# Graph kernel on one core: the first layer's segment sums with 64-column one-hot weights in two column tiles, edge values streamed, sums transposed back, and both one-hots from one operation

## What is computed

```python
z2 = jnp.concatenate([node_feat[src], node_feat[dst], edge_feat], axis=-1)
e = jax.nn.relu(z2 @ W_pre + b_pre)                 # 128 values an edge
deg = jax.ops.segment_sum(jnp.ones((e.shape[0],), e.dtype), dst, num_segments=N)
s = jax.ops.segment_sum(e, dst, num_segments=N)
mean_sq = jax.ops.segment_sum(e * e, dst, num_segments=N) / safe_deg
mx = jax.ops.segment_max(e, dst, num_segments=N)
mn = jax.ops.segment_min(e, dst, num_segments=N)
```

## Time and profile before

| | |
|---|---|
| median of 3 runs | 7895.94 us (7865.68 to 7899.78) |
| the profiled execution's own time | 7904.27 us, its span 7902.4 us |
| TensorE matmul busy | 5956.0 us (75%) |
| TensorE weight load busy | 5083.7 us (64%) |
| VectorE busy | 4835.5 us (61%) |
| ScalarE busy | 2658.9 us (34%) |
| GpSimd busy | 3831.2 us (48%) |
| mean granted TensorE clock | 0.79 |
| DMA | 541.35 MB |

### The profile page before, as it was taken

How to read it: one execution, slowest core, us unless ns; L and a number is a source line. 1 busy time by engine, 2 the same in 40 slices (tenths; PEclk the granted TensorE clock), 3 DMA queues, 4 the chain that set the end, 5 groups by cost and what they waited for, 6 DMA issues and landing times. The chain is left out here.

```text
span 7902.4 us, 163825 instructions
## 1 busy us (share of the span) xinstructions
PE 5956.0 (75%) x38014; PEld 5083.7 (64%) x38014; DVE 4835.5 (61%) x13892; ACT 2658.9 (34%) x5907; POOL 3831.2 (48%) x3975
## 2 busy tenths in 40 slices
PE   4888888888888888856767665667777676766674
PEld 4888888888888888435655553555555555555554
DVE  4666666666666666655555454556655565555557
ACT  1333333333333333212222233333333333333335
POOL 3455555545554544035555524555555555555552
PEclk7999999999999999968888776665666666666666
DMA  5444444444444444311111111111111111111111
GB/s 130 110 111 110 109 109 110 111 109 109 110 111 109 109 110 107 94 44 39 40 39 38 37 30 37 36 39 37 38 37 39 37 38 37 38 37 37 37 39 42
DMA packets 608470, 541.35 MB, mean 69 GB/s; under 512 B 307553, under 2 KB 485930, under 8 KB 608081
## 3 DMA queue, kind: packets, MB, share of 16 engines
q0 software_dynamic: 126192, 261.30, 13.9%
q1 hardware_dynamic: 356874, 163.66, 9.0%
q10 hardware_dynamic: 125272, 115.10, 5.5%
HBM read 517.22 MB, written 22.31 MB: 68 GB/s over the span
## 5 line engine op out<-in xcount | busy, mean ns | idle before, releaser
L1674 POOL DMA_INDIRECT Gt<-TAB,metat x1632 | 1586.4, 972 | 1522.5 <-DMA ad<-ADT 751.7
L520 POOL DMA_INDIRECT G<-Atab,meta x1616 | 1529.3, 946 | 1534.8 <-DVE EE L555 831.2
L659 PE MATMUL S<-oh,EE 128*128 128x64 f32 x6464 | 824.7, 280 | 218.7 <-DVE acc L586 110.8
L659 PEld LDWEIGHTS S<-oh,EE 128*128 128x128 f32 x6464 | 779.4, 196 | 283.1 <-DVE acc L586 155.6
L1166 POOL DMA_INDIRECT Gc<-XS,metac x672 | 650.0, 967 | 576.9 <-PE Sc L1336 294.5
L624 ACT COPY BS<-BK 128x512 f32<-128x512 f32 x404 | 237.0, 587 | 1861.5 <-PE BK L669 1630.5
L680 PE MATMUL S<-ohl,BS 128*128 128x64 f32 x6464 | 783.6, 274 | 6.2 <-issue 4.0
L680 PEld LDWEIGHTS S<-ohl,BS 128*128 128x128 f32 x6464 | 775.4, 195 | 13.6 <-issue 12.2
L555 DVE TENSOR_TENSOR EE<-Z,G 128x512 f32<-128x512 f32 x404 | 279.4, 692 | 783.6 <-remote 747.5
L1869 PE MATMUL SR<-P,Gt 128*128 128x128 f32 x3264 | 746.5, 400 | 0.0
L1869 PEld LDWEIGHTS SR<-P,Gt 128*128 128x128 f32 x3264 | 636.9, 291 | 114.7 <-issue 114.7
(11 more groups left out here) (269 smaller groups left out, 11712.6 us busy)
## 6 DMA issues: line engine op xcount, KB each, us to landing
mm<-MM ACTq DMA_DIRECT2D x404, 256.0 KB
ZR<-in_eft SPq DMA_DIRECT2D x404, 128.0 KB
dstb<-in_lin SPq DMA_DIRECT2D x404, 128.0 KB
Gt<-TAB,metat POOLq DMA_INDIRECT x1632
G<-Atab,meta POOLq DMA_INDIRECT x1616
ad<-ADT SPq DMA_DIRECT2D x816, 0.2 KB
WB<-Btab SPq DMA_DIRECT2D x404, 32.0 KB
Gc<-XS,metac POOLq DMA_INDIRECT x672
```

The costliest lines, as they stand in the source:

```text
L520: e.indirect_dma_start(G[:, k, s, :], None, Atab, bass.IndirectOffsetOnAxis(ap=meta[:, k, s:s + 1], axis=0)).then_inc(l_g[k], 16)
L659: mm = e.matmul(S1[:, a * W:(a + 1) * W], lhs, rhs, start=(s == 0), stop=(s == 3))
L1674: e.indirect_dma_start(G[:, k, s, :], None, TAB, bass.IndirectOffsetOnAxis(ap=meta[:, k, s:s + 1], axis=0)).then_inc(l_g[k], 16)
```

## The change

The one-hot becomes the stationary operand (64 columns) and 128 edge values are streamed. The values' sums go to partitions 0 to 63 of PSUM and the squares' to 64 to 127, as do the maximum and minimum, so two column halves of the array are used in turn. The results then have nodes on the partitions; ScalarE copies them to `SN1`/`SN2` (`e1`, `e2`), TensorE transposes them back (`t1`, `t2`), and VectorE adds the transposed block to `acc` as before. The one-hot of last edges comes from a number that the setup writes to a new table `MD`: the destination, lowered by 65536 where the next edge has the same one. One operation (`hot`, 512 columns) then makes both one-hots. `meta` is loaded in two parts. The order of stages changes on VectorE, ScalarE and TensorE, and `p4` moves from lag 6 to lag 5.

```diff
@@ setup, ScalarE
                                 vo[0:n, :, :]).then_inc(p_vo, 16)
+                    e.dma_start(MD[g * 128:g * 128 + n, :, :], mc[0:n, g % 2, :, :]).then_inc(p_md, 16)
                     if g < 2:
+                        e.wait_ge(p_md, 16 * (g + 1))
                         chunks(g + 2)
@@ setup, VectorE, each of four groups
+                    eq = hl[0:n, 0, :].rearrange("c (p s) -> c p s", s=4)
+                    ch(e.tensor_tensor(eq, mc[0:n, q, :, 4:8], mc[0:n, q, :, 8:12], ALU.is_equal))
+                    ch.sync()
+                    ch(e.scalar_tensor_tensor(mc[0:n, q, :, 8:12], eq, -65536.0, mc[0:n, q, :, 4:8],
+                                              ALU.mult, ALU.add))
@@ loads, SyncE
                 if not j.first(4):
-                    wait_sync(e, l_g[k], before[0], s_sync)
-                    wait_sync(e, s_d1, before[1], s_sync)
-                e.dma_start(meta[:, k, :], src[0]).then_inc(l_mt[k], 16)
+                    wait_sync(e, l_g[k], gathered, s_sync)
+                e.dma_start(ms[:, k, :], src[0]).then_inc(l_ms[k], 16)
...
+                if not j.first(4):
+                    wait_sync(e, s_zr, done, s_sync)
+                e.dma_start(dstb[64:128, k, :], src[4]).then_inc(l_db[k], 16)
+                if not j.first(4):
+                    wait_sync(e, s_oh, done, s_sync)
+                e.dma_start(md[:, k, :], src[1]).then_inc(l_md[k], 16)
@@ VectorE
-            def last(j):
+            def hot(j):
                 k = j.slot(4)
+                wait(e, l_md[k], 16 * j.uses(4))
                 if not j.first(4):
                     wait(e, s_p4, j.at(-3))
-                wait(e, s_d1, j.at(1))
-                e.tensor_tensor(ohl[:, k, :, :], oh[:, k, :, :], neq[:, k, :].unsqueeze(2).to_broadcast([128, 4, W]),
-                                ALU.mult).then_inc(s_ohl, 1)
+                e.scalar_tensor_tensor(oh[:, k, :, :], iotaW[:, :].unsqueeze(1).to_broadcast([128, 8, W]),
+                                       baseF[:, ds(j.at(), 1)],
+                                       md[:, k, :].unsqueeze(2).to_broadcast([128, 8, W]),
+                                       ALU.add, ALU.is_equal).then_inc(s_oh, 1)
...
-            pipeline(e, T, U, D, [(7, d4b), (2, d2), (0, d1), (3, last), (4, d4a), (4, d3)])
+            pipeline(e, T, U, D, [(2, d2), (0, d1), (6, d4b), (4, d4a), (2, hot), (4, d3)])
@@ ScalarE: e1 and e2 are new, the cast of oh comes last in a1
+                e.copy(SN1[:, :], S1[:, 0:128]).then_inc(s_e1, 1)
...
+                e.copy(SN2[:, :], S2[:, 0:128]).then_inc(s_e2, 1)
-            pipeline(e, T, U, D, [(5, a2), (1, masks), (2, a1)])
+            pipeline(e, T, U, D, [(5, a2), (1, masks), (2, a1), (3, e1), (5, e2)])
@@ TensorE
-                for a in range(3):
-                    for s in range(4):
-                        lhs = EE[:, q, a, s * 128:(s + 1) * 128] if a < 2 else onesb[:, :]
-                        rhs = oh[:, k, s, :] if a < 2 else ohb[:, q, s, :]
-                        mm = e.matmul(S1[:, a * W:(a + 1) * W], lhs, rhs, start=(s == 0), stop=(s == 3))
+                for s in range(4):
+                    e.matmul(S1[:, 256:256 + W], onesb[:, :], ohb[:, q, s, :], start=(s == 0), stop=(s == 3))
+                for s in range(4):
+                    for a in range(2):
+                        mm = e.matmul(S1[a * 64:(a + 1) * 64, 0:128], oh[:, k, s, :], EE[:, q, a, s * 128:(s + 1) * 128],
+                                      start=(s == 0), stop=(s == 3))
...
+            def t1(j):
+                wait(e, s_e1, j.at(1))
+                e.transpose(S1[:, 128:256], SN1[:, :], ident[:, :]).then_inc(s_t1, 1)
...
-            pipeline(e, T, U, D, [(5, p3), (1, p1), (6, p4), (3, p2)])
+            pipeline(e, T, U, D, [(5, p3), (6, t2), (4, t1), (1, p1), (3, p2), (5, p4)])
```

More of the change, by code:

```diff
@@ L440, in phase_l0 @@
         EE = sbt(ph, "EE", [128, 2, 2, CH])
-        oh = sbt(ph, "oh", [128, 4, 4, W])
+        oh = sbt(ph, "oh", [128, 4, 8, W])
         ohb = sbt(ph, "ohb", [128, 2, 4, W], BF16)
-        ohl = sbt(ph, "ohl", [128, 4, 4, W])
-        neq = sbt(ph, "neq", [128, 4, 4])
-        iob = sbt(ph, "iob", [128, 2, W])
         ST = sbt(ph, "ST", [128, 2, 2, CH])
         BS = sbt(ph, "BS", [128, 2, 2, CH])
+        SN1 = sbt(ph, "SN1", [128, 128])
+        SN2 = sbt(ph, "SN2", [128, 128])
         Z = [pst(ph, f"Z{k}", [128, CH]) for k in range(2)]
@@ L452, in phase_l0 @@
         BK = [pst(ph, f"BK{k}", [128, CH]) for k in range(2)]
-        S1v = S1[:, 0:3 * W].rearrange("p (a n) -> p a n", a=3)
-        S2v = S2[:, 0:2 * W].rearrange("p (a n) -> p a n", a=2)
+        S1v = S1[:, 128:128 + 3 * W].rearrange("p (a n) -> p a n", a=3)
+        S2v = S2[:, 128:128 + 2 * W].rearrange("p (a n) -> p a n", a=2)
         l_we = sem("l_we")
-        l_mt = [sem(f"l_mt{k}") for k in range(4)]
+        l_ms = [sem(f"l_ms{k}") for k in range(4)]
+        l_md = [sem(f"l_md{k}") for k in range(4)]
         l_in = [sem(f"l_in{k}") for k in range(4)]
@@ L474, in phase_l0 @@
         s_p4 = sem("l_p4")
+        s_e2 = sem("l_e2")
+        s_t2 = sem("l_t2")
         s_d4a = sem("l_d4a")
@@ L493, in loads @@
                 e0 = c * CH
-                src = (d["meta"][ds(c, 1), :, :].rearrange("a p s -> (a p) s"), d["eft"][:, ds(e0, CH)],
+                src = (d["meta"][ds(c, 1), :, 0:4].rearrange("a p s -> (a p) s"),
+                       MD[ds(c, 1), :, 4:12].rearrange("a p s -> (a p) s"), d["eft"][:, ds(e0, CH)],
                        Btab[ds(b, 64), :], d["lin"][ds(e0 + 1, CH)].partition_broadcast(64))
-                before = 64 * j.uses(4, -1), j.at(-3)
+                gathered, done = 64 * j.uses(4, -1), j.at(-3)
                 if not j.first(4):
-                    wait_sync(e, l_g[k], before[0], s_sync)
-                    wait_sync(e, s_d1, before[1], s_sync)
-                e.dma_start(meta[:, k, :], src[0]).then_inc(l_mt[k], 16)
+                    wait_sync(e, l_g[k], gathered, s_sync)
+                e.dma_start(ms[:, k, :], src[0]).then_inc(l_ms[k], 16)
                 if not j.first(4):
[L502 to L505, removed]
+                    wait_sync(e, s_p1, done, s_sync)
+                e.dma_start(ZR[0:64, k, :], src[2]).then_inc(l_in[k], 16)
+                e.dma_start(WB[64:128, k, :], src[3]).then_inc(l_in[k], 16)
+                if not j.first(4):
[4 more added lines that the diff above has]
+                e.dma_start(md[:, k, :], src[1]).then_inc(l_md[k], 16)
             pipeline(e, T, U, D, [(0, loads)])
@@ L514, in gather @@
                 k = j.slot(4)
-                wait(e, l_mt[k], 16 * j.uses(4))
+                wait(e, l_ms[k], 16 * j.uses(4))
                 if not j.first(4):
@@ L531, in d1 @@
             def d1(j):
-                k, q = j.slot(4), j.slot(2)
-                e.tensor_scalar(iob[:, q, :], iotaW[:, :], baseF[:, ds(j.at(), 1)], None, ALU.add).then_inc(s_iob, 1)
+                k = j.slot(4)
                 wait(e, l_db[k], 16 * j.uses(4))
@@ L538, in d1 @@
                                 ALU.subtract, ALU.is_equal).then_inc(s_zr, 1)
[L539 to L548, removed]
             def d2(j):
@@ L601, in a1 @@
                 q = j.slot(2)
[L602 to L605, removed]
                 wait(e, s_d2, j.at(1))
@@ L608, in a1 @@
                 wait(e, s_r, j.at(1))
-                e.activation(EE[:, q, 1, :], EE[:, q, 0, :], ACT.Square).then_inc(s_a1, 1)
+                e.activation(EE[:, q, 1, :], EE[:, q, 0, :], ACT.Square)
+                wait(e, s_oh, j.at(1))
+                if not j.first(2):
+                    wait(e, s_p2, j.at(-1))
+                e.copy(ohb[:, q, :, :], oh[:, j.slot(4), 0:4, :]).then_inc(s_a1, 1)
             def masks(j):
@@ L625, in a2, with e1, e2 @@
                 e.copy(BS[:, q, 1, :], BK[1][:, :]).then_inc(s_a2, 1)
-            pipeline(e, T, U, D, [(5, a2), (1, masks), (2, a1)])
+            def e1(j):
+                wait(e, s_p2, j.at(1))
+                if not j.first(1):
+                    wait(e, s_t1, j.at())
+                e.copy(SN1[:, :], S1[:, 0:128]).then_inc(s_e1, 1)
+            def e2(j):
+                wait(e, s_p4, j.at(1))
+                if not j.first(1):
+                    wait(e, s_t2, j.at())
+                e.copy(SN2[:, :], S2[:, 0:128]).then_inc(s_e2, 1)
+            pipeline(e, T, U, D, [(5, a2), (1, masks), (2, a1), (3, e1), (5, e2)])
         @blk.tensor
@@ L674, in p4, with t2 @@
                 wait(e, s_a2, j.at(1))
-                wait(e, s_ohl, j.at(1))
                 if not j.first(1):
                     wait(e, s_d4b, j.at())
-                for a in range(2):
-                    for s in range(4):
-                        mm = e.matmul(S2[:, a * W:(a + 1) * W], BS[:, q, a, s * 128:(s + 1) * 128], ohl[:, k, s, :],
+                for s in range(4):
+                    for a in range(2):
```

(6 more changed lines are left out.)

21 lines of the change are left out of this document (13 added, 8 removed).

## The result

The change took 8194.09 us (median of 4 runs, 8175.8 to 8212.37) against 7886.94 us for the kernel before: a ratio of 1.0392, 95% interval 1.0355 to 1.0429. The profiled execution took 8175.8 us, 271.5 more than the one before. The first and the last gather of the layer tell where they went.

What follows compares the result with a forecast made beforehand. Taken as bound: GpSimd's gathers holding back TensorE's completions, 7.39 us a job. The profiled 7904.27 us plus 20 (clock) and 10 (setup) gave 7934, or 7926 with the runs' median 8.3 lower; range 7750 to 8200 us.

Steps and rivals of the forecast that it cites:

- the forecast of no change: Likeliest case: the loop's step of 7.4 us stays, 7926 us in all, own range 7845 to 8005; chance 0.52.
- Rival 2: SyncE's queue becomes the bound: one more DMA issue makes 0.45 us a job, 182 us, about 8110 us; chance 0.20.
- The bound: In the loop, TensorE's completions reach other engines only after GpSimd's gathers are over; inferred from coincidences in time.
- the ring of gathers and release: Loop cycle: `d2` 0.69 us, 0.80 to GpSimd's start, gathers 4.70, release 1.2; 7.39 us a job.
- Sums on TensorE: Tile sums with 64-column weights save 1.0 us a job of TensorE's time, ends 0 and 2.0.
- All of it is beside the ring: TensorE's balance, 0.6 us more to 1.4 less a job, is costed at nothing in the loop's time.
- When the sums end: Sums on TensorE end +3.96 us after the release with overlap, 1 us later without; taken as still held by gathers.
- VectorE, ScalarE, setup, clock: VectorE's new operation 0.8 us, net 0.27 less; ScalarE's copies 0.6 a job; setup 10 us; lower TensorE clock 20 us.
- SyncE: One more DMA and wait in its queue cost 0, as it works ahead; other end 0.45 us a job.
- Rival 3: Jobs held twice: new hand-overs between ScalarE, TensorE and VectorE miss releases; 0.3 us a job, about 8050 us; chance 0.08.

Runs made afterwards that it cites:

- nogather_before: The kernel before without the gathers of the first layer: 7107.51 us against 7728.61 in one run, second chip.
- gather_p2_before: The kernel before, with GpSimd's gather of job k also waiting for `s_p2` of job k-5: 7545.38 us, 0.9764 times before.
- md_late: The changed kernel with the load of `md` one job later in SyncE's queue: 5996.17 us, 1.0038 times before, first chip.
- before_wait: The kernel before with one wait, for `s_ohl` of the job five earlier, at the end of SyncE's turn: 5972.11 us, 0.9998, first chip.
- md_act: The changed kernel with the load of `md` and its wait moved from SyncE's to ScalarE's queue: 7923.17 us, 1.0064 times before.
- serial: md_late with the two loops of the tile sums exchanged, values first, squares after: 5997.03 us, 1.0039 times before, first chip.
- md_lag2: md_late with the load of `md` two jobs later in SyncE's queue instead of one: 7840.03 us, 1.0166 times before.
- after_again: The changed kernel as it is, timed again on the second chip: 7994.98 us, 1.0333 times before.
- md_late_again: md_late unchanged, timed again on the second chip: 7847.57 us, 1.0145 times before.
- md_act_gather: md_act with the gather also waiting for `s_p2` of job k-5: 7725.98 us, 0.9817 times before.

## Why the prediction was right in part and wrong in its likeliest case

The range held the time by 6 us at its edge, and that is luck: the forecast of no change was wrong, and what came is the second rival, whose own time of 8110 us was 84 us too low.

- **The bound.** Right on chips with the long time: the ring of gathers and release, shown by nogather_before and by gather_p2_before. Not seen: that it isn't a property of the kernel. On the first chip of the experiments `d2` follows at once and the steps are 5.8 us. What sets them there wasn't tried; it isn't TensorE's busy time alone, since md_late has the same step with 1322 of 1600 us busy where before_wait has 1600.
- **Sums on TensorE.** Mis-sized: 1.0 us a job was taken as saved, with 2.0 as the end. The end was right, since 16 records take 1.10 us where they took 2.00. The earlier trace rows had no partner in the other column half and misled. The Trainium skill ("TensorEngine Tiling (Array Packing)", Performance Considerations and, for the rate, Overview) gives up to twice the rate for this swap; 0.125 against 0.068 us agrees. The wrong size cost the sum nothing, because the step "All of it is beside the ring" held: md_act saves 0.7 us a job of TensorE's busy time (2096 / 358 = 5.85, from 6.6) and gains nothing. (serial gives 1.02 back and loses nothing, but on the quick chip, where there is no ring.)
- **When the sums end.** Right: 3.6 us behind `d2` (forecast 3.96), and held wherever the gathers start in time, as in the timeline of md_act below. Where `ms` makes them late, the same 3.6 us end in the first 1.5 us of a run, and the job gets out.
- **VectorE, ScalarE, setup, clock.** `hot` takes 0.75 us (0.8 taken), the setup 7.6 (10 taken), the clock is 0.89.
- **SyncE.** This is the step that failed: "I take 0, since this queue works for jobs ahead of their use". That reason was true of the waits before, for `d1` and `p1`, which do a job two turns and one turn ahead of its `d2`; `meta` was issued 9 us ahead of its gather. The added wait is for `hot`, which stands in the same turn as `d2` and ends 2.9 us behind its start, and the next job's `ms` stands behind it in the queue. From there to that job's gather the ring leaves 7.35 - 2.9 + 0.69 + 0.78 = 5.9 us. In the trace `ms` is issued under 2.3 us behind the end of `hot` in the quickest tenth of the jobs and over 4.5 in the slowest, and lands 2.4 us later: 4.7 to 6.9 us, on both sides of the 5.9. What the wait costs alone on a chip with the long time wasn't tried.
- **Rival 2** had the right place and the right condition ("as soon as a full turn of the queue takes longer than 7.4 us"), which md_lag2 met to the letter. Its price of 0.45 us a job counted only the issue of one DMA. Measured are 0.67. Of the 3.3% of after_again, taking `md` and its wait off SyncE's queue removes 2.7 (after_again to md_act, on two chips). How that divides is less sure: md_late_again took away 1.9 by the place of the wait, though it made the queue longer by three instructions, and 0.8 more went with the queue's length (md_late_again to md_act). The last 0.6 is the setup and what stays open. What the price left out is that a late `ms` doesn't delay one gather by 0.4 us but tips two jobs into a pair, such as the one of 5.19 and 13.67 us.
- **Rival 3**, jobs held twice by the new hand-overs: not so in the change, by md_act, which has them all and 15 long steps like the kernel before. Pairs of that kind exist, but late `ms` makes them. Only in md_act_gather does the question stay open.

## What to carry to other kernels

Before a wait is added to a queue, ask in which turn of the other engine, and where in it, the awaited operation stands, and what is issued behind the wait: here a wait for a stage one or two turns ahead of `d2` left `meta` 9 us of lead, and one for a stage behind `d2` left `ms` 2.4. Count the queue's instructions a turn as well as its waits, since a queue can be the bound with no wait in it. And a saving on the busiest engine is worth nothing until the ring that sets the step has been found; removing one member of it (here the gathers) for a single run tells more than busy shares do.

## What the runs showed of the hardware that had not been expected

- The same program took 5973 us on one chip and 7729 to 7887 on others. Why the chips differ, no run shows. On the quick one completions of TensorE reach the other engines while gathers run (md_late's timeline above). On the others those that come 2 us or more into a run of gathers don't, as in this timeline of md_act, where sums that end at 1505.28 are copied at 1509.12, 1.2 us after the last gather:

```profile
1504.19 1.09 PE L682 MATMUL S<-EE,oh 128*64 128x128 f32 x16
...
1506.97 0.94 POOL L536 DMA_INDIRECT G<-Atab,ms  x1 [0.31 <-issue]
...
1509.12 0.27 ACT L642 COPY SN<-S 128x128 f32<-128x128 f32 x1 [3.57 <-remote]
```

- On those chips about a fifth of the steps in SyncE's queue take some 0.7 us while gathers run, as the issue of `ms` at 1109.33 above (0.70 us, 0.33 otherwise).
- The order of the column halves matters: 0.065 us a record when they alternate, 0.099 when four of one half are followed by four of the other.
- Gathers that run beside the 512-column `hot` take up to 1.5 us instead of 0.95; beside the 256-column `ohl` of gather_p2_before up to 1.2.
